# Two-layer FFN kernel: the second layer's first 20 convolution units among the first layer's last products, x1 turned with z, and output scattered by rows

## The reference, cut to what matters

```python
# layer 0: a per-batch 128 x 128 mix of channels, then a 2048 x 2048 linear map with a low-rank update
x = x + _L0_ffn_ref(_L0_cond_ref(x, cond_128, ...), ...)
# layer 1: grouped convolution (4 groups of 32 channels, 9 taps), then a gathered FFN per head
out = lax.conv_general_dilated(x, weight, ..., feature_group_count=4) + ctx + bias
t = out.reshape(b * l, 2048)[:, perm].reshape(4096, 16, 128)
t = gelu(einsum('bhd,hdm->bhm', t, up))      # up:   16 x 128 x 512
t = einsum('bhm,hmd->bhd', t, down)          # down: 16 x 512 x 128
x = x + t.reshape(4096, 2048)[:, argsort(perm)].reshape(32, 128, 2048)
```

## Time and profile before

| | |
|---|---|
| median of 3 runs | 2505.79 us (2500.85 to 2511.16) |
| the profiled execution | 2513.49 us, span 2511.7 us |
| mean granted PE clock | 0.989 |
| PE busy | 2432.4 us (97% of the span) |
| VectorE, ScalarE, GpSimd busy | 1713.9, 1113.7, 938.1 us |
| DMA | 540.90 MB, mean 215 GB/s |

### The profile page before, as it was taken

One profiled execution on the slowest core, in us unless ns is written; L12 is line 12 of the kernel. 1 busy time (PEld: TensorE's weight loads), 2 busy tenths in 40 slices (PEclk: granted clock), 3 DMA queues, 4 the chain that ended last, 5 costly groups with the idle time before them and its releaser, 6 DMA issues.

```text
span 2511.7 us, 37065 instructions
## 1 busy us (share of the span) xinstructions
PE 2432.4 (97%) x11130; PEld 2010.9 (80%) x11130; DVE 1713.9 (68%) x2449; ACT 1113.7 (44%) x1850; POOL 938.1 (37%) x826
## 2 busy tenths in 40 slices
PE   8899999999999999999999988999999999999985
PEld 6788888888888888887888866888888888888864
DVE  6665555875555855558544665778888888888865
ACT  3221211321212322223222356777777777777753
POOL 2275654556645255323233311222222222222331
PEclk9999999999999999999999999999999999999988
DMA  8965554755543767657555665468888888888898
GB/s 301 326 214 187 199 174 159 258 177 205 202 163 132 269 219 225 204 178 258 178 172 172 194 196 153 141 189 244 242 245 248 240 240 243 245 246 245 231 245 255
DMA packets 397563, 540.90 MB, mean 215 GB/s; under 512 B 37016, under 2 KB 262640, under 8 KB 397360
## 3 DMA queue, kind: packets, MB, share of 16 engines
q1 hardware_dynamic: 295872, 309.50, 43.0%
q10 hardware_dynamic: 77376, 152.17, 16.2%
q0 software_dynamic: 24112, 76.80, 9.9%
HBM read 309.72 MB, written 228.61 MB: 214 GB/s over the span
## 4 chain that ended last, share of the span: by engine, by line
PE 88%; DMA 5%; DVE 3%; issue 2%; SPq 1%; ACT 1%; POOL 0%; ACTq 0%; DVEq 0%; POOLq 0%
PE ps_c L463 45%; PE ps_up L1401 13%; PE ps_y L1411 13%; PE ps_c L1426 9%; PE ps_v L441 4%; PE ps_c L429 3%; DMA u_s<-z_d,idx 1%; DVE w_lo L1006 1%; PE ps_up L1426 1%; SPq L88 1%; DMA rear<-x_d 1%; DVE ring_lo L953 1%; DMA w_hi<-y_d 1%; DMA x_n<-in_up 0%; DVE x_s L1002 0%
## 5 line engine op out<-in xcount | busy, mean ns | idle before, releaser
L463 PE MATMUL ps_c<-w_hi,ring_hi 128*128 128x512 f32 x1792 | 703.9, 393 | 4.9 <-DVE r_early L1002 3.6
L463 PE MATMUL ps_c<-w_hi,ring_lo 128*128 128x512 f32 x1792 | 698.0, 390 | 0.0
L463 PE MATMUL ps_c<-w_lo,ring_hi 128*128 128x512 f32 x1792 | 697.9, 389 | 0.0
L613 ACT ACTIVATE ring_hi<-raw_n 128x512 fp32r<-128x512 f32 x382 | 239.6, 631 | 852.2 <-DVE raw_n L944 232.1
L1581 DVE TENSOR_TENSOR g_lo<-kern,g_hi 128x512 fp32r<-128x512 f32 x512 | 349.2, 687 | 80.3 <-ACT g_hi L1483 71.3
L463 PEld LDWEIGHTS ps_c<-w_hi,ring_hi 128*128 128x128 f32 x1792 | 336.8, 188 | 75.8 <-DVE ring_lo L953 4.7
L463 PEld LDWEIGHTS ps_c<-w_hi,ring_lo 128*128 128x128 f32 x1792 | 336.5, 188 | 69.8
L463 PEld LDWEIGHTS ps_c<-w_lo,ring_hi 128*128 128x128 f32 x1792 | 336.8, 188 | 67.5
L1383 POOL DMA_INDIRECT y_d<-y_room,idx x128 | 131.8, 1030 | 651.7 <-ACT y_room L1516 584.9
L1002 DVE TENSOR_TENSOR r_early<-ps_c,r_early 128x512 f32<-128x512 f32 x256 | 176.4, 689 | 275.9 <-PE ps_c L463 275.9
L1479 ACT ACTIVATE kern<-ps_up 128x512 f32<-128x512 f32 x512 | 304.5, 596 | 118.4 <-PE ps_up L1401 102.8
(11 more groups left out here) (188 smaller groups left out, 3628.0 us busy)
## 6 DMA issues: line engine op xcount, KB each, us to landing
u_d<-raw_n ACTq DMA_DIRECT2D x64, 512.0 KB, 3.2
x_d<-r_early ACTq DMA_DIRECT2D x128, 256.0 KB, 3.5
raw_n<-u_d SPq DMA_DIRECT2D x64, 512.0 KB, 3.6
x_d<-x_s ACTq DMA_DIRECT2D x126, 256.0 KB, 2.8
u_s<-x_d SPq DMA_DIRECT2D x496, 64.0 KB, 2.4
z_d<-x_s SPq DMA_DIRECT2D x120, 256.0 KB, 4.7
rear<-y_d SPq DMA_DIRECT2D x224, 128.0 KB, 3.7
rear<-x_d SPq DMA_DIRECT2D x56, 512.0 KB, 4.4
```

Source lines behind the costliest of these rows:

```text
L463: mm = nc.tensor.matmul(bank, a[:, dc, :], w[k][:, dc, :], start=(first and dc == 0 and n == 0), stop=(dc == 3 and n == 2), skip_group_che ...
L613: nc.scalar.activation(ring_hi[g % RING][:].rearrange("p a n -> p (a n)"), factor(q, k, p), ACT.Copy).then_inc(hi_ready, 1)
```

## The change

**Lead.** The 20 leading units go into the first layer. `conv_slot(u)` puts unit u behind item 359 + 17u/4, one unit for 4.25 items from item 359 to item 439; they use two PSUM banks that `make_u` no longer needs. The kernel's own weights are split in quad 24 (`split_kernel`), not at the end. SP loads a unit's rows two units ahead and stores x1 and z tiles behind items 375, 392, 409, 426 and 443.

**x1 by rows.** Each unit's x1 rows are turned too (`turn_x`, VectorE), stored to xt_d in the layout of z_d (`store_x`), and gathered by POOL with the same index (`gather_row`). VectorE adds PSUM and the gathered row (`add_rows`) in place of ScalarE's copy, and POOL scatters the sum straight to the output, whose rows the host puts in order. y_d, its reload, the second load of x1, the turn of y, the separate sum, the output stores by SP and the whole end stage are gone. There is one tile for turned x1 and, in the second layer, one for turned z.

**Weights.** Instead of 24 chunks by four stages, the last quad brings six loads of four chunks each (1 MB), straight to where the lo parts will be; 18 chunks are split there by ScalarE and VectorE, the other 14 in steps 0 to 13, one each, hi on ScalarE and lo on GpSimd. The GELU table is loaded at the start of the last quad.

**Casts and code.** ScalarE now makes three of the four GELU casts and VectorE one. All 128 steps are written out. The four loads of a unit's x1 rows were issued by SP before the change and still are; in the step that stores, they now stand behind the eight stores.

In the diff's two functions `step`, the first is SyncE's and the second GpSimd's.

```diff
@@ -70,23 +65,112 @@
+    def load_rows(self, eng, x1_d, u):
+
+        tile = u // SB
+        b, g = SB * (tile // G) + u % SB, tile % G
+        wait(eng, self.xlo_ready, u - 1)
+        wait(eng, self.xt_ready, u - 1)
...
+def conv_slot(u):
+
+    return 25 * ITEMS + 9 + 17 * u // 4
+
+
+def load_slot(u):
+
+    return conv_slot(u - 2) if u >= 2 else 25 * ITEMS + 4
...
             def slot(q, t):
                 product(q, t)
+                for u in units(conv_slot, q, t, 0):
+                    if u < LEAD:
+                        conv(u)
...
+                for u in units(load_slot, q, t, 0):
+                    sh.load_rows(sp, x1_d, u)
+                for u in units(conv_slot, q, t, 4):
+                    if u < LEAD and u % SB == SB - 1:
+                        sh.store_x(sp, xt_d, u)
+                        sh.store_z(sp, z_d, u)
...
+            def load_early(k):
+                pool.wait_ge(item_mm, ITEMS * (QUADS - 1) + 2 * k + 2)
+                pool.dma_start(sh.w_raw[k][:], up_down[:, 4 * k:4 * (k + 1), :]).then_inc(sh.w_in[k], 16)
...
                 if q == QUADS - 1 and t == 2:
-                    for n in range(4, EARLY):
-                        load_early(n)
+                    gather_t(0)
+                    load_early(0)
+                    load_early(1)
+                if q == QUADS - 1 and t == 6:
+                    gather_row(0)
+                    gather_row(1)
+                    load_early(2)
+                    gather_t(1)
+                    for k in range(3, 6):
+                        load_early(k)
...
         def by_scalar(mc):
-
-            return mc % 2 == 0
+            return mc != 1
...
+            def step(u, s):
+                if LEAD <= u < STEPS and u % SB == SB - 1:
+                    store_x(u)
+                    store_z(u)
+                if LEAD + 2 <= u + 2 < STEPS:
+                    sh.load_rows(sp, x1_d, u + 2)
...
+            def step(u, s):
+                if s + 3 < STEPS:
+                    gather_t(s + 3)
+                if 2 <= s + 2 < STEPS:
+                    gather_row(s + 2)
+                if s in (1, 2):
+                    load_weights(s + 5)
+                for n in chunk_split_in(s):
+                    split_weights(n)
+                if s == 0:
+                    pool.wait_ge(sh.idx_ready, BLOCKS - 1)
+                if s >= 0:
+                    scatter(s)
...
+            def add_rows(s):
+                dve.wait_ge(down_done, MC * (s + 1))
+                dve.wait_ge(row_in[s % 4], 16 * (s // 4 + 1))
+                nc.vector.tensor_tensor(rows[:, s % 4, :], ps_y[s % 2][:, 0, :], rows[:, s % 4, :], ALU.add).then_inc(o_ready, 1)
```

More of the change, by code:

```diff
@@ L43 @@
 QUADS = 32
-EARLY = 24
+EARLY = 18
 ITEMS = 14
@@ new lines, in store_tile, with store_z @@
+    def store_tile(self, eng, dram, turned, tile, stored):
+        for r in range(S):
+            rows = dram[tile // G % 2].rearrange("(w i r) n -> r i w n", w=WIDE, r=S)
+            eng.dma_start(rows[r, :, :, tile % G * C:(tile % G + 1) * C],
+                          turned[r * GC:(r + 1) * GC].rearrange("p w b c -> p w (b c)")).then_inc(stored[tile % 2], 16)
+    def store_z(self, eng, z_d, u):
+        eng.wait_ge(self.zt_ready, u + 1)
+        self.store_tile(eng, z_d, self.z_tile(u // SB), u // SB, self.z_out)
@@ new lines, in store_x, with tile_free, block_stored, gather @@
+    def store_x(self, eng, xt_d, u):
+        eng.wait_ge(self.xt_ready, u + 1)
+        self.store_tile(eng, xt_d, self.x_tile, u // SB, self.xt_out)
+    def tile_free(self, eng, stored, tile):
+        if tile > 0:
+            eng.wait_ge(stored[(tile - 1) % 2], 64 * ((tile - 1) // 2 + 1))
+    def block_stored(self, eng, stored, s):
+        if s % H == 0:
+            for j in range(2):
+                eng.wait_ge(stored[j], 64 * 2 * (s // H + 1))
+    def gather(self, pool, out, dram, s, arrived):
+        pool.indirect_dma_start(out=out, out_offset=None, in_=dram[s // H % 2],
+                                in_offset=bass.IndirectOffsetOnAxis(ap=self.idx[:, 0, s % H:s % H + 1], axis=0)).then_inc(arrived, 16)
@@ L279, in mix_count, with units @@
             return 8 * sweep(q) + 2 * (q % 8 - 1)
+        def units(place, q, t, shift):
+            return [u for u in range(LEAD + 2) if place(u) + shift == ITEMS * q + t]
         def quads(slot, first=0):
@@ L1327, in _, with store_z, store_x @@
-            sp.wait_ge(sh.pad_ready, 7)
-            load_x1(-2, 2 * H - LEAD + 3)
-            sh.store_last()
-            drive(sp, step)
-            finish()
-            for v in range(H):
-                store_last(sp, v, range(2))
-            sp.wait_ge(o_out, 16 * PAIRS * (BLOCKS - 1))
+            def store_z(u):
+                tile = u // SB
+                if tile % G == 0:
+                    wait(sp, tlo_ready, H * (tile // G - 1))
+                sh.store_z(sp, z_d, u)
+            def store_x(u):
+                tile = u // SB
+                if tile % G == 0 and tile // G >= 2:
+                    for j in range(4):
+                        sp.wait_ge(row_in[j], 16 * (H // 4) * (tile // G - 1))
+                sh.store_x(sp, xt_d, u)
@@ L1455, in _ @@
+            drive(step)
         @block.scalar
@@ L1520, in _, with step @@
-            drive(act, step)
-            for v in range(H):
-                store_last(act, v, range(2, SB))
-            act.wait_ge(last_o_out, 64 * H)
+            def step(u, s):
+                if s >= 0 and s + 2 < STEPS:
+                    split_t(s + 2)
+                if LEAD <= u < STEPS:
+                    take_z(u)
+                if LEAD < u + 1 < STEPS:
+                    split_x(u + 1)
+                for n in chunk_split_in(s):
+                    split_weights(n)
+                for mc in range(MC):
+                    if s + 1 < STEPS:
+                        gelu(s + 1, mc)
@@ L1626, in build @@
     z_d = [scratch(f"z_d{j}", [L, RB]) for j in range(2)]
-    y_d = [scratch(f"y_d{j}", [L, RB]) for j in range(2)]
+    xt_d = [scratch(f"xt_d{j}", [L, RB]) for j in range(2)]
     with ExitStack() as ctx:
```

786 lines of the change are left out of this document (312 added, 474 removed).

## The result

| | before | after |
|---|---|---|
| median | 2506.1 us (2500.85 to 2511.16, 4 runs) | 2538.16 us (2530.54 to 2542.62, 4 runs) |
| profiled execution | 2513.49 us, span 2511.7 | 2542.06 us, span 2540.3 |
| mean granted PE clock | 0.989 | 0.985 |
| DMA | 540.90 MB, 215 GB/s | 507.04 MB, 200 GB/s |

The ratio is 1.0124, with a 95% interval of 1.0107 to 1.014: slower by 1.2%, where 2438 us was forecast. I follow PE's times first, as the prediction did.

A forecast was written before the change was run, and what follows sets the result against it. The prediction took TensorE (PE) to bound the kernel. Losses of 83.9 us less 5 + 4 + 6.5 gave 68.4 us saved: 2445.1 us profiled, 2437.4 at the median, stated as 2438 us, range 2424 to 2472.

The forecast's parts named there:

- Bound by PE, a change wins where PE waits: Whole kernel: TensorE is the bound, so a change can only win where PE waits or runs at its low clock.
- The lead in the first layer at nothing: First layer: the 20 leading units cost their 41.8 us of products; their other work hides, costed at nothing.
- The border, 5 us: Between the layers: PE stalls 5 us, mainly for late weights, between 0 and the present 28.1.
- The end, 6.5 us: After the last product: drain 0.2, sum 0.69, issue 0.74, scatter's landing 4.44 and 0.4 for the rest, 6.5 us.
- The steps, 4 us: Second layer's 128 steps: PE stays the bound at 7.56 us per steady step, with 4 us of stalls in all.
- rival A: Storing steps: x1 rows come late behind the stores, PE stands 1.2 us at each of 27 tiles; 2470 us, chance 0.12.
- From the profiled execution to the median: Whole run: 2445.1 us by the profiled execution, which lay 7.7 us above the median, gives 2437.4, stated as 2438.
- Rows of x1 by SyncE cost nothing by themselves: x1 row loads: SP already issued them before, so this costs and gives nothing; only their place behind the stores is new.
- B: Border: it stays as long as today, gathers waiting behind the 1 MB loads; +23, 2461 us, chance 0.10.
- C: Steps 0 to 13: GpSimd's subtractions hold VectorE up, 1.09 us each, all reaching PE; +15, 2453 us, chance 0.06.
- D: Every second-layer step: a third indirect DMA on POOL's queue delays z gathers, 0.5 us each; +64, 2502 us, chance 0.05.
- Rival E: Second-layer tiles: VectorE's turn waits for the store from the one turned-x1 tile, 4 us each; 2546 us, chance 0.05.

The follow-up runs named there:

- kernel 1: Changed kernel, but in the storing step SyncE issues the x1 loads between the x1 stores and the z stores; 2447.8 us, ratio 0.9768.
- experiments 1 and 3: Changed kernel with x1 loads between x1 and z stores: 2447.8 us; kernel before with second-layer z stores ahead of x1 loads: 2584.0 us.
- experiment 8: Changed kernel, but in the storing step SyncE issues x1 loads, then z stores, then x1 stores last; 2649.37 us, ratio 1.0568.

## Why the prediction was wrong

**Bound by PE, a change wins where PE waits.** Right. (The low slices of the earlier trace rows are the 24th and 25th, 1444 to 1570 us, and not 27 and 28; the windows had the border at the right place.) PE has 96% of the span, and kernel 1 shows what it is with PE's wait gone.

**The lead in the first layer at nothing.** Right within 1.8 us: PE waits 2.4 us once for the split of a leading unit (ps_v for xp_lo). The x1 turn stood 12.9 us there, in 3 times, for the store of the tile before.

**The border, 5 us.** 2.6 us of wait, and the first nine products of the second layer take 3.7 us instead of 2.1, at a granted clock of 0.54; that share stands in the 99.

**The end, 6.5 us.** It took 9.1. The sum (0.70) and the scatter's issue (0.97, from 2532.37) are as taken within 0.3 us; from the issue's end at 2533.34 to the end of the span are 7.0 us, where the 4.44 of the earlier trace rows and 0.4 had been taken. The DMA view has the scatter's data moved by 2534.7; no row shows what the rest is.

**The steps, 4 us.** This failed: 99 us. The busy sums were near: in kernel 1 VectorE's 161.48 of 200 us are 6.1 of 7.56, as forecast, and ScalarE's 160.28 are 6.1 too, with 5.8 forecast; no engine reaches 7.56. What fails is rival A, which I had named with the right place and order and put aside at 0.12:

- *The sizes of its terms.* I took the loads' issue from an undisturbed row, 2.3 us, and their landing from the page's median, 2.4. Behind the z stores they are 3.4 and 4.18 us, and the z stores 5.15, not 3.86. The sum is 16.4 us, not 12.1. The trace of before had the row that I needed, loads directly behind z stores:

```profile
1923.87 3.88 SPq L1305 DMA_DIRECT2D z_d<-x_s  x4
1928.00 4.27 SPq L88 DMA_DIRECT2D u_s<-x_d  x4
```

- *Who waits.* I compared the landing with the time when ScalarE wants the rows (10.4 us) and let ScalarE's 1.8 us of spare time absorb the difference. But the conv unit is the first work of its step on PE, and a split that comes late is late for PE itself; ScalarE's spare time lies behind it. The right bound was PE's 15.1 us less the two splits: 13.7. By it the 12.1 of my sum would have had 1.6 us of room, and 16.4 are 2.7 us late, as measured.
- *The price.* 1.2 us per tile gave 2470. The medians of the kernel after and of kernel 1 differ by 90.4 us, 3.3 per tile. The traces show of what: a wait of 2.6 (66.5 / 26), and 1.1 (29.9 / 27) of slower products, for which the price had no term. Together they make up the 95.1 us between the spans of the two profiled executions.

**From the profiled execution to the median.** Without the failed step the sum was good. Kernel 1 loses 17.5 us where 15.5 had been taken (3.5 to its first `up` at 1505.4, 4.9 in the second layer, 9.1 at the end), so the sum foretells its span within 2 us. But I then took off 7.7 us, because the profiled execution of before lay that far above its median. Kernel 1's lies at its own median (2447.0 and 2447.8), so it looks as if the excess belonged to what the old execution lost, and went with it; no run shows where that execution lost it. 2438 was 9.8 us too low even for the case that I forecast: 7.7 by this step, 2 by the terms.

**Rows of x1 by SyncE cost nothing by themselves.** Right as far as it went: SP is the best issuer of the three ways tried. The place behind the stores is the loss, as the experiments 1 and 3 show from both sides.

**The rivals B, C and D** did not come: the border cost 2.6 us, and gathers of z made ScalarE wait 31.7 us in 39 times and PE never. Of C only the seed was there: VectorE was held, but it had the time to spare. These are g_lo on VectorE from 1506 to 1620 us, and the weights' subtraction on GpSimd (count, then ns min/median/max):

```profile
L1491 DVE TENSOR_TENSOR g_lo<-kern,g_hi x52: 672/691/2961, 1510.5 to 1617.0; 128x512 fp32r<-128x512 f32 x52
```

```profile
L1325 POOL TENSOR_TENSOR w_lo<-w_raw,w_hi x14: 1274/1302/1451, 1515.5 to 1634.4; 128x512 fp32r<-128x512 f32 x14
```

PE waited 0.4 us for it, once. The longest of them, and the GpSimd operation beside it:

```profile
1532.29 2.96 DVE L1491 TENSOR_TENSOR g_lo<-kern,g_hi 128x512 fp32r<-128x512 f32 x1
```

```profile
1533.37 1.32 POOL L1325 TENSOR_TENSOR w_lo<-w_raw,w_hi 128x512 fp32r<-128x512 f32 x1
```

VectorE began 1.08 us earlier and still ended 0.56 us after GpSimd. So it is with all 14: the VectorE subtraction that overlaps one of them ends 0.55 to 0.58 us behind it, whichever began first. So VectorE lost up to 2.3 us at one of them, where my price for C had 1.09. None that overlaps a gather or scatter alone took over 0.75 us. The Trainium skill's rule (SBUF — State Buffer, section SBUF: two separate sides) gives the shared port to the one of the two that starts first, for its whole length. The trace agrees that VectorE is held to the end of GpSimd's subtraction. In 9 of the 14 VectorE had begun first, by the recorded starts (those on GpSimd are rough), and was held all the same; GpSimd was then still at a gather or scatter. What holds VectorE before the subtraction begins is not shown.

**Rival E** stayed out in this order: in the second layer VectorE never waited for the store of turned x1. My price of 4 us per tile was too low for where it does decide: 7.5 in experiment 8 (2649.4 us against the 2447.8 of kernel 1).

## What to carry to other kernels

In a queue that issues in order, a load that feeds the bottleneck goes ahead of a store that must wait for its data; ask of each moved DMA what stands ahead of it and when the first of these can go. Reckon the deadline back from the bottleneck engine's own start, not from a helper's idle share, and take issue and landing times from rows with the same neighbours in the queue. A small room per step is a threshold: on one side it costs nothing, on the other it costs the excess, plus slower products after some of the waits.

## What the runs showed of the hardware

- Issuing is not cheap, and depends on what goes before and beside it. Four loads of 64 KB took SP 2.25 us in an undisturbed stretch, 3.4 to 4.3 directly behind stores; ScalarE issued four in 1.8 us, but took 3.07 for two while SP issued stores. The Trainium skill (DMA: Bandwidth & Descriptors, section Issuing engines are not separate DMA queues) calls the time that it takes to initiate a DMA "usually small relative to the DMA itself". Here one load took 0.4 to 1.6 us to issue, against 4.18 us until the last had landed, and the issues of a queue add up: 8.6 us for four stores and four loads. That is not small, and the measurement decides.
- After a wait, PE can be slower for a while. Nine products took 2.09 us with no wait, and 2.36 after one of 2.78 us, at a granted clock of 1.00. In experiment 8 they took 4.11 us behind a wait of 5.35, and in another tile of the kernel after 4.00 behind one of 4.04 (to the start of the tenth product), both at 0.50, the 1.2 GHz level. The two tiles of the kernel after (window, us, PE, PEld, DVE, ACT, POOL busy, PE clock, DMA share, GB/s):

```profile
1931.53:1933.89 2.36, 2.36 (x10) 1.95 (x11) 1.86 (x4) 2.33 (x5) 0.00 (x0) 1.00 0.00 0
2064.94:2068.94 4.00, 4.00 (x9) 3.14 (x10) 3.50 (x7) 3.60 (x7) 0.00 (x0) 0.50 0.00 0
```

Of the 26 conv units behind a wait in the kernel after, 12 took 3.0 to 4.0 us from their first product to the start of the tenth and 14 took 2.2. The waits before the slow ones were 1.86 to 6.36 us long, those before the others 0.78 to 3.05, so the length of the wait alone does not decide. The mean granted clock of the windows from 1900 to 2100 us was 1.00 in kernel 1, 0.97 in the kernel after and 0.91 in experiment 8.
- Less DMA traffic (507.04 MB for 540.90) gave no shorter landings for the loads that mattered; another order did (4.18 us behind four z stores, 1.9 behind two).
